# Cross-attention outputs of a decoder kernel: divided unit by unit on Pool, and projected beside the last unit's values

## What is computed

```python
y = jnp.einsum('bhqk,bhkd->bhqd', jax.nn.softmax(att, axis=-1), v)          # own keys, causal
...
y = y + jnp.einsum('bhqk,bhkd->bhqd', jax.nn.softmax(attc, axis=-1), vc)    # 1601 context keys
y = y.transpose(0, 2, 1, 3).reshape(x.shape[0], T, C)
return y @ Wp + bp
...
x = _layernorm(x + _L0_xattn_ref(x, ctx_512, ...), axis=-1)
```

## Time and profile before

| | |
|---|---|
| time, three runs | 791.42 us median (791.12 to 796.45) |
| profiled execution | 791.42 us, span of its trace 789.3 us |
| busy in the span | PE 638.6, DVE 534.3, ACT 428.5, POOL 163.7 us |
| first blocks (loads, self-attention, splitting) | to about 100 us |
| a middle unit | 18.7 us |
| last values of the last unit end | 399.9 us |
| second residual sum R ends | 435.7 us |
| normalised X of this block ends | 441.1 us |

### The profile page before, as it was taken

The page is one execution under the profiler, slowest core; times in us unless marked ns, Lnnn a source line. Parts: engine busy times, 40 slices in busy tenths (PEclk is TensorE's granted clock), DMA queues, the critical chain, the costliest instruction groups (busy, mean ns, idle before and its releaser), DMA issues. The chain is left out here.

```text
span 789.3 us, 13349 instructions
## 1 busy us (share of the span) xinstructions
PE 638.6 (81%) x5152; PEld 350.2 (44%) x5152; DVE 534.3 (68%) x683; ACT 428.5 (54%) x774; POOL 163.7 (21%) x164
## 2 busy tenths in 40 slices
PE   7979398989999999999969477897404789877996
PEld 5546133333333333333323245684201466655884
DVE  5458688888999999999223489896488343426442
ACT  3556078788888888888930133455730212234323
POOL 6336333340000000000013095000150280003100
PEclk9999689999999999999975688999855879999999
DMA  7045666442111111100030056540000300000000
GB/s 185 32 127 202 196 207 191 158 168 88 48 49 49 50 53 54 53 31 2 9 91 1 2 209 150 182 152 0 0 0 0 147 0 1 1 0 1 1 0 27
DMA packets 31978, 57.58 MB, mean 73 GB/s; under 512 B 6584, under 2 KB 22848, under 8 KB 31472
## 3 DMA queue, kind: packets, MB, share of 16 engines
q1 hardware_dynamic: 26960, 31.84, 13.0%
q0 software_dynamic: 4352, 22.69, 8.4%
q10 hardware_dynamic: 608, 2.25, 1.3%
HBM read 38.18 MB, written 16.49 MB: 69 GB/s over the span
## 5 line engine op out<-in xcount | busy, mean ns | idle before, releaser
L834 ACT ACTIVATE prob<-ps 128x512 f32<-128x512 f32 (+2 forms) x480 | 252.4, 582 | 61.9 <-PE ps L657 54.9
L956 DVE TENSOR_REDUCE pm<-ps 128x2 f32<-128x1024 f32 x192 | 226.1, 1221 | 19.6 <-PE ps L619 17.8
L657 PE MATMUL ps<-qq,kc 50*128 50x256 bf16 (+1 forms) x832 | 136.6, 279 | 9.8 <-DMA qq<-mrow 9.8
L680 PE MATMUL ps<-prob,vst 128*9 128x256 f32 (+1 forms) x1664 | 130.2, 385 | 8.8 <-ACT o_all L822 8.8
L619 PE MATMUL ps<-kc,qq 48*128 48x512 bf16 x384 | 119.9, 402 | 6.6 <-DVE pm L956 3.7
L657 PEld LDWEIGHTS ps<-qq,kc 50*128 50x128 bf16 (+1 forms) x832 | 53.1, 97 | 105.3 <-ACT prob L834 72.9
L1078 POOL TENSOR_TENSOR y<-y 128x256 f32<-128x256 f32 x16 | 11.4, 722 | 243.1 <-issue 228.4
L680 PEld LDWEIGHTS ps<-prob,vst 128*9 128x9 f32 (+1 forms) x1664 | 25.2, 89 | 50.5 <-ACT prob L834 36.6
L963 DVE TENSOR_REDUCE nm<-ps 128x4 f32<-128x512 f32 (+1 forms) x32 | 30.6, 958 | 14.5 <-PE ps L607 14.4
L619 PEld LDWEIGHTS ps<-kc,qq 48*128 48x128 bf16 x384 | 33.6, 95 | 15.3 <-DVE pm L956 9.4
L1770 ACT ACTIVATE prob<-s 128x512 f32<-128x512 f32 (+1 forms) x28 | 15.5, 566 | 45.3 <-PE s L1708 45.3
(11 more groups left out here) (346 smaller groups left out, 1261.4 us busy)
## 6 DMA issues: line engine op xcount, KB each, us to landing
kc<-kc_scr SPq DMA_DIRECT2D x32, 150.1 KB
comb_bc<-comb_scr SPq DMA_DIRECT2D x8, 512.0 KB, 4.8
kc<-kc_scr SPq DMA_DIRECT2D x32, 100.1 KB
raw<-in_wexp POOLq DMA_DIRECT2D x8, 384.0 KB, 7.4
exp_scr<-raw_high POOLq DMA_DIRECT2D x8, 384.0 KB, 4.1
exp_scr<-raw_low POOLq DMA_DIRECT2D x8, 384.0 KB, 6.7
up_high<-exp_scr SPq DMA_DIRECT2D x8, 256.0 KB, 2.7
up_low<-exp_scr SPq DMA_DIRECT2D x8, 256.0 KB, 2.8
```

The source lines that it names most:

```text
L657: last = pe.matmul(bank[0:p, j * TQ:(j + 1) * TQ], kc[s][rows, j, t * 128:t * 128 + p], qq[s][rows, 0, j, :], start=(j == 0), stop=True, s ...
L680: last = pe.matmul(o_ps[32 * hh:32 * hh + VW, kind * TQ + q0:(kind + 1) * TQ], value[:, hh * VW:(hh + 1) * VW], prob[0:k, (NST * n + t) % ...
L834: act.activation(prob[0:p, g % P_RING, 2 * e:2 * e + 2, q0:TQ], s2[0:p, k % S2_RING, 0:2 * w].rearrange("p (i q) -> p i q", i=2), ACT.Exp, ...
L956: dve.tensor_reduce(pm[:, m % 2, c, :, jt], banks, AX.X, ALU.max).then_inc(s1_read, 1)
```

## The change

The division moves into the units, and the projection into the attention block.

- SP, in its round m: the transfer of unit m-1's denominators into a small tile of 128 x 16 (`denominators_out`), of unit m-3's reciprocals to DRAM (`reciprocals_out`, ahead of the loads) and back into 128 partitions, each row read by 32 of them (`reciprocals_back`, behind the loads).
- DVE: the reciprocal of 128 x 16 for unit m-3 after the maximum of half 5 of unit m; no splitting into bf16 parts.
- POOL, behind the experts' split: for each unit but the last the product with the spread reciprocals (128 x 512) and the sum of both halves (128 x 256), in place in `o_all` (`normalise`).
- PE: the projections of units 0 to 10 in steps 4 to 14 of the last unit, those of 11 to 14 behind its values. The last unit's denominators are spread by one f32 matmul over the accumulator's copy itself (`spread` now has its ones in the denominators' rows), and DVE takes the reciprocal of 128 x 512 from PSUM, multiplies and adds, before the last projection. DVE adds both chunks of R (`projected`) in this block.
- The next block begins with the norm. The tiles `xk` and `xq` get their own memory; the new tiles lie in the tile `below`.

```diff
@@ SP
+                    def denominators_out(n):
...
+                        sp.wait_ge(o_copied, n + 1)
+                        if n >= 2:
+                            sp.wait_ge(rden_done, n - 1)
+                        sp.dma_start(den[:, n % 2 * DEN:(n % 2 + 1) * DEN], o_all[HD:128:32, n, :]).then_inc(den_in[n % 2], 16)
+                    def reciprocals_out(n):
+                        sp.wait_ge(rden_done, n + 1)
+                        sp.dma_start(rden_scr[n].rearrange("h (p k) -> (h p) k", k=DEN),
+                                     rden_u[:, n % 2 * DEN:(n % 2 + 1) * DEN]).then_inc(rden_out, 16)
+                    def reciprocals_back(n):
+                        sp.wait_ge(rden_out, 16 * (n + 1))
+                        if n >= 2:
+                            sp.wait_ge(y_scaled, n - 1)
+                        sp.dma_start(den_bc[:, n % 2, :],
+                                     rden_scr[n].unsqueeze(1).to_broadcast([4, 32, 2 * TQ])).then_inc(bc_in[n % 2], 16)
...
+                        if m >= 3:
+                            reciprocals_out(m - 3)
+                        if n < NU:
                             load_context(n)
                             for kind in X_KINDS:
                                 load_split(kind, n)
-
-                    sp.wait_ge(o_copied, NU - 1)
-                    sp.dma_start(den[:, 0, :], o_all[HD:128:32, 0:NU - 1, :]).then_inc(den_in, 16)
-                    sp.wait_ge(den_done, 5)
-                    for part in range(3):
-                        sp.dma_start(rden_rows[4 * part:4 * part + 4, 0:NU - 1, :], den_part[:, part, :]).then_inc(rden_in, 16)
-                    sp.wait_ge(rden_in, 48)
+                        if m >= 3:
+                            reciprocals_back(m - 3)
+                        if m:
+                            denominators_out(m - 1)
+                    for n in (NU - 3, NU - 2):
+                        reciprocals_out(n)
+                        reciprocals_back(n)
@@ POOL
+                    def normalise(n):
+                        pool.wait_ge(bc_in[n % 2], 16 * (n // 2 + 1))
+                        pool.tensor_tensor(o_all[:, n, :], o_all[:, n, :], den_bc[:, n % 2, :], ALU.mult).then_inc(y_scaled, 1)
+                        pool.wait_ge(y_scaled, n + 1)
+                        pool.tensor_tensor(o_all[:, n, 0:TQ], o_all[:, n, 0:TQ], o_all[:, n, TQ:2 * TQ], ALU.add).then_inc(ys, 1)
...
+                    for n in range(NU - 1):
+                        normalise(n)
@@ PE
+                    def project(n):
...
+                        pe.wait_ge(*((ys, n + 1) if n < NU - 1 else (last_y, 2)))
+                        last = pe.matmul(ps[:, 4 + b // 2, (b % 2) * TQ:(b % 2 + 1) * TQ], later["wp"][:, g, :], o_all[:, n, 0:TQ],
+                                         start=(g == 0), stop=(g == NG - 1))
+                        if n % 8 == 7:
+                            last.then_inc(proj, 1)
                     for g in range(NU * NST):
                         scores_and_half(g, g + HALVES + S1_LEAD)
                         if g >= 2:
                             outputs((g - 2) // NST, (g - 2) % NST)
+                        if g >= (NU - 1) * NST + 4:
+                            project(g - (NU - 1) * NST - 4)
                     for t in (NST - 2, NST - 1):
                         outputs(NU - 1, t)
+                    for n in range(NST - 4, NU - 1):
+                        project(n)
+                    pe.wait_ge(o_copied, NU)
+                    pe.matmul(ps[:, 6, :], later["spread"][:], o_all[:, NU - 1, :], start=True, stop=True).then_inc(last_bc_ps, 1)
+                    project(NU - 1)
@@ DVE
+                            if m >= 3 and i == 5:
+                                reciprocals(m - 3)
...
                     row(NU - 1)
-                    dve.wait_ge(den_in, 16)
-                    reciprocals(dve, den, den_part, den_done)
+                    for n in (NU - 3, NU - 2):
+                        reciprocals(n)
+                    projected(0)
+                    o = o_all[:, NU - 1, :]
+                    dve.wait_ge(last_bc_ps, 1)
+                    dve.reciprocal(last_bc, ps[:, 6, :]).then_inc(last_y, 1)
+                    dve.wait_ge(last_y, 1)
+                    dve.tensor_tensor(o, o, last_bc, ALU.mult).then_inc(y_scaled, 1)
+                    dve.wait_ge(y_scaled, NU)
+                    dve.tensor_tensor(o[:, 0:TQ], o[:, 0:TQ], o[:, TQ:2 * TQ], ALU.add).then_inc(last_y, 1)
+                    projected(1)
@@ emit_rest, the block behind: the loop over 16 units on PE, DVE and POOL is gone
-                for n in range(NU):
-                    b, g = n // NG, n % NG
-                    if n + 2 < NU:
-                        denominators(n + 2)
-                    pe.wait_ge(ys, n + 1)
...
+                dve.sem_inc(r_ready, NCH)
                 dve_ln(0)
                 dve_ln(1)
```

More of the change, by code:

```diff
@@ L978, in row, with reciprocals, projected @@
                                           ALU.subtract).then_inc(mrow_ready, 1)
+                    def reciprocals(n):
+                        at = slice(n % 2 * DEN, (n % 2 + 1) * DEN)
+                        dve.wait_ge(den_in[n % 2], 16 * (n // 2 + 1))
+                        if n >= 2:
+                            dve.wait_ge(rden_out, 16 * (n - 1))
+                        dve.reciprocal(rden_u[:, at], den[:, at]).then_inc(rden_done, 1)
+                    def projected(c):
+                        at = slice(c * CH, (c + 1) * CH)
+                        dve.wait_ge(proj, c + 1)
+                        dve.scalar_tensor_tensor(out=R[:, at], in0=ps[:, 4 + c, :], scalar=col["bp"], in1=X[:, at],
+                                                 op0=ALU.add, op1=ALU.add).then_inc(b3_r, 1)
                     for m in range(NU):
@@ L1062, in _ @@
                     load_down(sp, s, s)
-                sp.wait_ge(den_done, 5)
-                for part in range(3):
-                    sp.dma_start(rden_rows[4 * part:4 * part + 4, NU - 1, :], den_part[:, part, :]).then_inc(rden_in, 16)
                 sp.wait_ge(comb_sb, 2)
```

91 lines of the change are left out of this document (25 added, 66 removed).

## The result

The changed kernel takes 799.2 us (median of 20 runs, 795.8 to 802.6), the kernel before 795.8 us on the same chip (20 runs, 790.8 to 801.4). The ratio is 1.0049, 95% interval 1.0030 to 1.0069: no gain, half a per cent lost, where 2.3% were forecast. The forecast was counted from 791.42 us, the median of three runs, which is 4.3 us under the median of the twenty. The profiled execution took 799.48 us (span 797.2) at the same mean clock as before, 0.903.

A forecast was written before the change was run, and what follows sets the result against it. PE, DVE and ACT nearly full in the units, then 35.78 us of serial work. Units +1.3 + 0.3, last unit +3.4, tail -26.2, norm +3.3: -17.9, from 791.4 to 773.5 us; range 768.5 to 780 us.

The forecast's parts named there:

- the tail: Last values to R: 9.6 us, between 9.0 and 10.6, in place of 35.8, so -26.2 us.
- the serial loop: Behind the units: one loop per unit over DVE, POOL and PE, 35.78 us up to R, which the change takes apart.
- The last projection: In the new tail, after PE idles over 4.6 us: runs at half clock and takes 1.2 us.
- The norm: R to X: 8.7 us for 5.4, +3.3; means at half clock, variances at full; 7.0 to 10.1 us.
- The last unit: Eleven projections at 0.48 us in steps 4 to 14 make PE the bound: +3.4 us, between 2.6 and 5.2.
- The units: DVE's reciprocals add 1.3 us (0 to 3.1), SP's three new transfers 0.3 us (0 to 0.8).
- 1.8 us of slack: SP's queue in a unit: max rows go out 0.1 to 0.3 us later, covered if landings take 1.93 us with issue.
- each microsecond of lateness would cost one microsecond: Max rows, if their cover were gone: price of lateness in each of ten units, 4 to 13.
- the early units: Cover already gone there: one new transfer ahead of unit 3's rows costs 0.3 us, between 0 and 0.8.
- DVE would not wait: Denominators in the units land by 248.6 us, DVE needs them at 252.4: 3.8 us free.
- rival C: SP's queue: max rows land over 6 us after issue, 2.6 us a unit, 26 us, 799.5 us; chance 0.03.
- Rival B: SP's queue: broadcast ahead of max rows uses their 1.8 us and 0.5 more, 5 us, 778.5 us; chance 0.10.

The follow-up runs named there:

- rows_first: Changed kernel with broadcast and denominators queued behind the max rows on SP, and DVE's reciprocal moved to half 12: 778.4 us, ratio 0.9773.
- all_proj_late: Changed kernel with the eleven projections moved from the last unit's steps to behind its values: 800.8 us, ratio 1.005.
- small_back: Changed kernel with the 256 KB broadcast replaced by 8 KB to 4 partitions, same place, units 0 to 14 not normalised: 777.3 us, ratio 0.9777.
- only_broadcast: Changed kernel keeping only the 256 KB broadcast, from input rows; both 64-byte transfers and DVE's reciprocals of units 0 to 14 left out: 790.3 us, ratio 0.9935.
- late_recip: Changed kernel with DVE's reciprocals behind half 12 of a unit in place of half 5: 801.3 us, ratio 1.0080.
- outer2: Changed kernel with the 256 KB broadcast reading 2 input rows, each copied 64 times (outermost dimension 2): 836.7 us, ratio 1.0498.

## Why the prediction was wrong

**What bounds the kernel, and the tail.** Right. Taking the serial loop apart gave -26.6 us for -26.2 forecast: 9.15 us from the last values to R for 9.6. The reciprocal of 128x512, priced from two other shapes at 3.4 us, took 3.36; the spreading matmul 1.02 for 1.07; the product 0.69. The four projections took 1.99 for 1.9. The last projection took 0.94, not 1.2: the clock was still granted at 0.87 in the stretch from 436 to 438 us. In rows_first, where it had fallen to 0.50 by 414 us, the same projection took 1.22.

**The norm.** 9.06 us for 8.7. The two windows:

```profile
436.00:438.00 2.00, 0.83 (x2) 0.30 (x2) 1.08 (x2) 0.00 (x0) 0.00 (x0) 0.87 0.00 0
438.00:444.00 6.00, 4.82 (x7) 2.04 (x7) 0.75 (x1) 2.48 (x3) 0.00 (x0) 0.50 0.55 158
```

The means ran at half clock as forecast; so did most of the first of the two variances, which I had at full. The range to 10.1 us held that.

**The last unit.** +5.5 us for 3.4, just outside 2.6 to 5.2. The mechanism (PE takes the bound from ACT, step by step) was right: a step takes 1.51 us in place of 1.01. The mis-sized term is the projection's 0.48 us, taken from projections back to back. Back to back it is 0.45 (all_proj_late); in a step, counting from the prediction's 0.88 without it, it is 1.51 - 0.88 = 0.63.

**The units: the step that failed.** "With such a landing about 1.8 us of slack stay, and 0.3 us is covered." The issue times in that step were right or high (0.35, 0.56 and 0.59 us for "about 0.6 each"). The landing was wrong. I took it for all three new transfers from the one row (1.93 us with its issue), a transfer of 8 KB on an empty queue, and left the 256 KB broadcast without a price of its own in this place. Its landing is late (8.7 us), and what counts, the max rows behind it are late too (8.3 us): +24.6 us for 1.6. Two smaller things were wrong in the same step. That "each microsecond of lateness would cost one microsecond" left out the half clock behind a long stop: 17.0 us lost for 12.4 us of waiting, from the sixth row on. And the early units, sized at 0.3 us and at most 0.8, lost 0.5 to 4.0 us before any broadcast. The sentence that DVE would not wait, "3.8 us are free. A landing of twice that length would do", fell with it: the denominators needed 8.2 us.

**The rivals.** It went the way of rival C, which I gave 0.03. Its condition was met, rows landing over 6 us after their issue (8.3 us). Its price was close (2.6 us in each of ten units, 26 us, 799.5 us in all; the runs show 24.6 and 799.2), but in part by luck: the loss is uneven, from nothing to 4.7 us a unit, and includes 4.0 us ahead of the first broadcast and the half clock, neither of which C had. Against it I had written that nothing in the middle units showed this. But the kernel before had no broadcast in its units, so its units could not show it. That argument was no evidence. Rival B named the transfer and priced it at 0.5 us a unit without working out why. What could have been worked out beforehand: the rule of the Trainium skill named above (the section on why a transfer counts 16) gives four engines for this source, and the DMA share of the earlier trace rows, 0.16 in a middle unit, already belonged to loads with 3 and 2 copies outermost, among others. I cited the same page for the fixed cost of a small transfer, which it gives for the path of transfers issued by GpSimd while these are SP's, and passed over this rule.

**With the broadcast out of the way the rest of the sum held.** small_back measures what else the change adds to the units: 1.2 us for 1.6. And rows_first, which is the change with that one fault mended, took 778.4 us beside 797.3 for the kernel before, a ratio of 0.9773: times 791.42 us that is 773.5 us (768.9 to 778.0), the forecast. That it agrees to the digit is luck, since the interval is 9 us wide. Its trace says the same more roughly: X ends at 424.30 us, 16.8 earlier than before, for 17.9 forecast.

**What stays open.** How the 11.8 us between only_broadcast (+12.8) and the changed kernel (+24.6) divide. Of these 3.7 arise before the fifth row (0.3 against 4.0), where traces of the same program differ by nearly as much. Of the other 8.1, DVE's own stop is at most 2.0 (late_recip, from the fifth row on); the rest goes with the denominators behind the broadcast and the reciprocals' issue ahead of the loads, which no run separates, and holds the half clock of the longer stops. Why single units escape the loss is open too. The last 1.0 us of the span's growth lies behind X, within the spread there.

## What to carry to other kernels

Before a transfer is put into a queue, ask for each one queued behind it how many DMA engines the new one uses: look at the outermost dimension of its source, the side that these runs varied, and put a stride-0 copy dimension outermost if it is the larger. Count the engine's lost clock as well as its wait. Put what another engine waits for first, and bulk traffic behind it, in the queue's idle time. And when the profile "shows nothing" of a danger, check whether the kernel before had anything in it that could have shown it; if not, price the danger from its mechanism.

## What the runs showed of the hardware that was not expected

- The same 256 KB to the same 128 partitions cost the units 2.4, 4.9, 24.6 or 55.6 us, by whether the source's outermost dimension was 32, 8, 4 or 2.
- A stop of PE costs more than its length: from the sixth row on, 12.4 us of waiting went with 6.2 us more for the same 2367 matmuls, and 32.9 us with 22.1 more, at mean granted clocks of 0.97 and 0.87 in place of 1.00.
- The time of an issue on SP is not fixed. The four max rows took 2.69 us in the unit shown with the small transfer, 3.98 in the unit shown of the changed kernel, but 2.70 in most units of only_broadcast, straight behind the broadcast, and 4.25 to 5.17 in three early units of small_back, with no broadcast at all. So the broadcast by itself does not set it, and what does was not separated. In outer2 one issue of 8 KB took 1.94 us in place of 0.59:

```profile
272.27 1.94 SPq L372 DMA_DIRECT2D below<-o_all  x1
```

- A projection of 256 columns in f32 takes 0.45 us behind its like; between matmuls of other shapes it adds 0.63 us to a step (the difference worked out above), at the same granted clock of 1.00.
